# The preparation of a graph kernel in another order: histogram of 64 by 98 columns, projection spread over the statistics, scaling and turning between its last tiles

## The chip, the core and the metric

One core of a Trainium2 chip runs the kernel. It has a matrix engine (TensorE, PE in the profile), a vector engine (DVE), a scalar engine (ACT), GpSimd (POOL), an engine that only issues transfers (SP), and 16 DMA engines. Each engine works through its own list of instructions in order and waits on semaphores for the others. The metric is the time of one execution on the device in microseconds (us), lower is better; the figure of a kernel is the median of its timed runs.

## The reference

Two blocks of a graph network over 6250 nodes with 256 features and 100000 edges (sorted by their destination) are computed, each behind a layer norm and with a residual. The first has three hops of graph convolution, the second two layers of attention with four heads.

```python
h = jnp.maximum(_layernorm(x, axis=-1), 0.0)
x = x + _L0_gnn_ref(h, L0_gnn_W, L0_gnn_b, src, dst)
h = jnp.maximum(_layernorm(x, axis=-1), 0.0)
x = x + _L1_gnn_ref(h, edge_index, L1_gnn_W1, ..., L1_gnn_b2)

# _L0_gnn_ref
out_deg = jax.ops.segment_sum(ones, src, num_segments=N)
in_deg = jax.ops.segment_sum(ones, dst, num_segments=N)
out_norm = jnp.clip(out_deg, 1.0, None) ** (-0.5)
in_norm = jnp.clip(in_deg, 1.0, None) ** (-0.5)
h = x
for i in range(3):
    h = h * out_norm[:, None]
    h = jax.ops.segment_sum(h[src], dst, num_segments=N)
    h = h * in_norm[:, None]
    h = h @ W[i] + b[i]
    if i < 2:
        h = jax.nn.relu(h)
```

The change is confined to what comes before the first hop: the out-degree of every node (a histogram of 100000 numbers), the layer norm of x, and the product of its rows with the first weights, which the kernel takes ahead of the hop (sum and product may be exchanged).

## The kernel before

**Stages.** The nodes are 49 tiles of 128 rows (`NT`). The preparation fills the table `conv_tab[0]` in device memory with the scaled and projected rows. A hop then gathers, for each of 782 chunks of 128 edges, one row per edge from the table (POOL, L643) into a ring of 64 places; PE multiplies each with a one-hot matrix of destinations (L1015), and DVE adds the product to the sums of a tile in `acc` (L1303). Two more hops, two attention layers and the output follow. The change leaves them as they are.

**The histogram.** The source number of an edge is split into a low and a high part: `lo` = number mod 128, `hi` = number / 128. 800 columns of 125 edges are worked through in 40 halves of 20 columns (`HB`). For a half DVE makes the one-hot rows of both parts (L1171, two instructions, 128x20 and 49x20 elements of bf16), in one of two buffers. PE then runs 20 products of bf16 into the accumulator `psad` (L922): for column j the stationary operand is `oh_lo[:, b, :, j]`, 128 columns, and the moving one `oh_hi[:, b, :, j]`, 49 columns. The last index is the fastest one in memory and has 20 places, so both operands are read with a step of 20 elements, 40 bytes. DVE may fill a buffer again when PE has read it (semaphore `hist_done`), PE waits for `hist_onehots`. The result lies as 128 x 49, which is the layout of the tiles.

**Layer norm and projection.** x lies in `acc` (as `xa`). Per tile ACT takes mean and square sum (L706, L711), POOL subtracts the mean and clips at zero (L619, semaphore `x_ready`) and between its rows issues 14 gathers of index rows (L613). PE turns the tile by two transposes (`turn`, L936), ACT copies the turned tile from PSUM (L696), PE multiplies it with the weights (`multiply`, L944, two products in fp32 that the chip runs as four passes), and ACT copies the result back to `xa` (L719, semaphore `staged`). In ACT's own list the two copies of tile t stand right behind the statistics of tile t+3 and t+4, so statistics and projection go at one pace.

**The order of PE.** It is written out by hand. `HIST_LEAD` = 6: after every pair of halves (40 products) come two tiles, from the fourth pair on. 34 tiles are turned inside the histogram, 15 behind it.

**Behind the last tile.** DVE forms the out-norm and the factor `oscale` (L1219 to L1224, ACT takes the square root, L724), multiplies the projected rows by it in seven blocks (L1228, semaphore `ln_rows`), and SP stores each block when it is ready (L438). Then DVE prepares the chunk rows (L1233 to L1238), PE turns 14 blocks of them (L982, L988) and DVE copies each (L1241, L1244), packs tile numbers (L1250) and raises `steps_ready` (L1256). POOL's first gather waits for `steps_ready` and for all seven stores (`table_stored`). DVE waits for the stores too, clears `acc` in seven pieces (L1259) and starts the first hop.

Of the kernel before, what the change touches and what calls it, by code (L numbers as in the profile page):

```python
# [14 lines left out]
BF16 = mybir.dt.bfloat16  # L15
I32 = mybir.dt.int32
ALU = mybir.AluOpType
# [33 lines left out]
HIST_LEAD = 6  # L51
# [17 lines left out]
assert LP * LC == E and LC % (2 * HB) == 0 and NT % TB == 0 and S % 8 == 0 and U > LAG + 1 and S >= EC + NT - 1  # L69


def gnn(nc, x, src, dst, gw, gb, w1, as1, ad1, b1, w2, as2, ad2, b2, out):
    ctx = ExitStack()
    with ctx:
# [123 lines left out]
        o_lo, o_hi = 4 * LC, 4 * LC + HB * P  # L198
        oh_lo = ring[:, o_lo:o_hi].bitcast(BF16).rearrange("p (b n k) -> p b n k", b=2, k=HB)
        oh_hi = ring[:, o_hi:o_hi + HB * NT].bitcast(BF16).rearrange("p (b n k) -> p b n k", b=2, k=HB)  # L200
        o_c = o_hi + HB * NT
        iota_lo = ring[:, o_c:o_c + HB * P // 2].bitcast(BF16).rearrange("p (n k) -> p n k", k=HB)
        o_c += HB * P // 2
        iota_hi = ring[:, o_c:o_c + HB * NT // 2].bitcast(BF16).rearrange("p (n k) -> p n k", k=HB)
        o_c += HB * NT // 2
# [26 lines left out]
        o_c += 8 * SB + P + 2  # L232
        assert o_c <= RING * AW
# [157 lines left out]
        def _(sp):  # L391
# [44 lines left out]
            for q in range(NI):  # L436
                sp.wait_ge(ln_rows, TB * (q + 1))
# [133 lines left out]
        def _(pool):  # L571
            chain = [0]

            def link(ins):
# [9 lines left out]
            link(nc.gpsimd.iota(iota_lo, pattern=[[1, P], [0, HB]], base=0, channel_multiplier=0,  # L584
                                allow_small_or_imprecise_dtypes=True))
            nc.gpsimd.iota(iota_hi, pattern=[[1, NT], [0, HB]], base=0, channel_multiplier=0,
# [6 lines left out]
                                         base=0, pattern=[[-1, P]], channel_multiplier=1))  # L593
            link(nc.gpsimd.memset(ones[:, :], 1.0))
# [84 lines left out]
        def _(act):  # L679
# [18 lines left out]
            for s in range(NT + 4):  # L698
# [10 lines left out]
                if 0 <= t < NT:  # L709
# [3 lines left out]
                t = s - 3  # L713
                if 0 <= t < NT:
                    copy_rows_T(0, t)
                t = s - 4
                if 0 <= t < NT:
                    act.wait_ge(projected, t + 1)
                    nc.scalar.copy(xa[:, t, :], main[2 + t % 2][:, 0:C]).then_inc(staged, 1)  # L719
            chain[0] += NT  # L720
# [5 lines left out]
            root(norms[:, :], 1)  # L726
# [183 lines left out]
        def _(pe):  # L910
            pe.wait_ge(consts, 2)

            nc.tensor.matmul(psad[:, 0:NT], zero_b, zero_b[:, 0:NT], start=True, stop=False,
# [3 lines left out]
            def hist(first, end):  # L917
                for i in range(first, end):
# [39 lines left out]
            for i in range(NH):  # L958
# [6 lines left out]
                for t in (2 * i - HIST_LEAD, 2 * i + 1 - HIST_LEAD):  # L965
                    if t >= 0:
                        turn(0, t)
                    if t >= 1:
                        multiply(0, t - 1, wc, C)
# [772 lines left out]
```

## Time and profile before

| | us |
|---|---|
| median of 3 timed runs | 5737.9 (5733.7 to 5739.26) |
| the profiled execution | 5745.21 |
| its span in the profile | 5743.4 |
| PE busy | 3964.7 (69%) |
| POOL busy | 4134.0 (72%) |
| DVE busy | 3730.1 (65%) |
| ACT busy | 2157.1 (38%) |

The span reaches from the first to the last instruction of the profiled execution; 1.8 us of its time lie outside it. The profiled execution took 7.3 us more than the median. The preparation is the first 200 us, or 3.5% of the span. PE and PEld are two rows of one engine, products and loads of the stationary operand. The end of a matmul in the profile is modelled, its start is recorded, so the pace of PE is read from starts. PEclk is the granted clock of TensorE as a share of 2.4 GHz: 1.00 is 2.4 GHz, 0.50 is 1.2 GHz, and values between are a mix of the two in time.

### The profile page before, as it was taken

What the parts mean: (1) busy time and instruction counts of PE and PEld (TensorE: products, weight loads), DVE (VectorE), ACT (ScalarE), POOL (GpSimd) and SP (SyncE); (2) the same over time, 40 slices, a digit from 0 to 9 for tenths busy, and PEclk for the clock granted to TensorE, in tenths of its full rate; (3) what the DMA queues carried; (4) which work ended last, traced back from release to release, by engine and by line L of the source; (5) the groups of instructions that cost most, each with busy time, mean ns of one, the idle gap of its engine ahead of it and who ended that gap; (6) DMA issues with size and microseconds to landing.
All of it is one profiled execution on the core that took longest, in us unless ns stands there. A gap on an engine that the chain in (4) does not pass through costs nothing.

```text
span 5743.4 us, 108186 instructions
## 1 busy us (share of the span) xinstructions
PE 3964.7 (69%) x15160; PEld 2622.1 (46%) x15160; DVE 3730.1 (65%) x12287; ACT 2157.1 (38%) x7129; POOL 4134.0 (72%) x4290
## 2 busy tenths in 40 slices
PE   8566666676666667566666677777787677777772
PEld 8344444453344445343443454554554445444441
DVE  6556555555555554555555567777777677777777
ACT  3100000020000002000000088888888488888883
POOL 4577777777777777777777647777775577777775
PEclk8778777788777778777777788888888788898886
DMA  2443333333333333433333354444443344444444
GB/s 68 115 112 105 106 106 105 106 106 105 106 105 106 105 106 99 131 106 106 105 106 105 114 157 109 110 109 110 109 110 87 121 110 110 110 110 110 110 109 145
DMA packets 311837, 627.27 MB, mean 109 GB/s; under 512 B 87063, under 2 KB 182511, under 8 KB 311182
## 3 DMA queue, kind: packets, MB, share of 16 engines
q0 software_dynamic: 192928, 530.18, 33.4%
q1 hardware_dynamic: 111902, 88.77, 5.0%
q8 instruction: 222, 3.64, 0.3%
q14 instruction: 401, 3.28, 0.2%
q10 hardware_dynamic: 6384, 1.39, 0.2%
HBM read 573.49 MB, written 47.33 MB: 108 GB/s over the span
## 4 chain that ended last, share of the span: by engine, by line
PE 35%; DVE 19%; DMA 18%; issue 12%; POOL 11%; DVEq 3%; ACT 1%; POOLq 0%; SPq 0%; ACTq 0%
PE main L1015 20%; DMA ring<-conv_tab,csrc 14%; DVE acc L1303 8%; POOL ring L643 7%; PE main L1119 6%; PE main L944 4%; DMA ring<-attn_tab,sidx 4%; POOL ring L655 3%; DVEq L1303 2%; DVE ring L1631 2%; PE pso L1038 1%; PE psad L922 1%; POOL ring L675 1%; PE pso L936 1%; DVE ad L1525 1%
## 5 line engine op out<-in xcount | busy, mean ns | idle before, releaser
L643 POOL DMA_INDIRECT ring<-conv_tab,csrc x2346 | 2231.1, 951 | 729.8 <-issue 467.1
L1303 DVE TENSOR_TENSOR acc<-acc,main 128x264 f32 (+2 forms) x4160 | 1764.9, 424 | 1365.8 <-PE main L1015 963.6
L1015 PE MATMUL main<-ring,oh 128*128 x4992 | 1900.1, 538 | 1074.6 <-SPq L453 751.3
L655 POOL DMA_INDIRECT ring<-attn_tab,sidx x1664 | 1603.8, 964 | 624.2 <-issue 364.7
L1015 PEld LDWEIGHTS main<-ring,oh 128*128 128x128 f32 x4992 | 1226.8, 267 | 1744.6 <-issue 1539.2
L1119 PE MATMUL main<-ring,oh 128*128 128x264 f32 x3328 | 1211.7, 475 | 112.1 <-ACT ring L867 102.1
L867 ACT ACTIVATE ring<-ring 128x64 f32<-128x64 f32 x3328 | 918.9, 345 | 0.0
L1295 DVE TENSOR_SCALAR oh<-iota,dloc 128x128 f32<-128x128 f32 x2505 | 768.0, 307 | 169.7 <-issue 104.7
L1119 PEld LDWEIGHTS main<-ring,oh 128*128 128x128 f32 x3328 | 592.8, 220 | 262.3 <-DVE ring L1631 185.5
L845 ACT ACTIVATE oh<-iota,dloc 128x128 f32<-128x128 f32 x1752 | 558.0, 396 | 5.1 <-DMA attn_tab<-oh 5.1
L1631 DVE TENSOR_TENSOR ring<-ring 128x128 f32<-128x128 f32 x1670 | 467.8, 285 | 0.1
L797 ACT ACTIVATE nb<-acc,stat 128x256 f32<-128x256 f32 x49 | 24.5, 501 | 994.8 <-DVE stat L1403 994.8
L783 ACT ACTIVATE nb<-acc,inorm 128x256 f32<-128x256 f32 x49 | 24.3, 498 | 993.6 <-DVE acc L1303 993.3
L724 ACT ACTIVATE sdeg<-sdeg 128x49 f32<-128x49 f32 x1 | 0.2, 245 | 1016.3 <-DVE sdeg L1359 1016.3
L1038 PE MATMUL pso<-ident,oh 128*128 128x128 f32 x1744 | 334.5, 324 | 16.9 <-issue 7.9
L1055 PE MATMUL psad<-tvb,ohT_room 128*128 x1728 | 310.4, 189 | 46.8 <-ACT ohT_room L833 14.3
L833 ACT CAST ohT_room<-pso 128x512 bf16<-128x512 f32 x436 | 252.1, 578 | 169.7 <-PE pso L1038 168.9
L853 ACT ACTIVATE oh<-oh,ones 128x512 f32<-128x512 f32 x438 | 314.5, 718 | 0.7
L1055 PEld LDWEIGHTS psad<-tvb,ohT_room 128*128 128x128 bf16 x1728 | 184.1, 107 | 216.9 <-issue 145.7
L1038 PEld LDWEIGHTS pso<-ident,oh 128*128 128x128 f32 x1744 | 223.6, 164 | 46.0 <-issue 12.1
L675 POOL TENSOR_TENSOR ring<-ring,es 128x256 f32<-128x256 f32 x98 | 120.8, 1270 | 92.9 <-DMA ring<-attn_tab 92.9
L944 PE MATMUL main<-wc,aT 128*128 128x256 f32 x588 | 167.3, 412 | 0.7 <-DVE aT L1331 0.6
(210 smaller groups left out, 2815.6 us busy)
## 6 DMA issues: line engine op xcount, KB each, us to landing
ring<-conv_tab,csrc POOLq DMA_INDIRECT x2346, 2.8
ring<-attn_tab,sidx POOLq DMA_INDIRECT x1664
conv_tab<-oh SPq DMA_DIRECT2D x14, 896.0 KB, 4.0
ring<-attn_tab SPq DMA_DIRECT2D x14, 896.0 KB, 7.2
flag_room<-start_rows SPq DMA_DIRECT2D x424, 8.0 KB
flag_room<-end_rows SPq DMA_DIRECT2D x424, 8.0 KB
attn_tab<-ring SPq DMA_DIRECT2D x7, 910.0 KB, 4.4
attn_tab<-oh SPq DMA_DIRECT2D x7, 910.0 KB, 4.3
```

The costliest lines, as they stand in the source:

```text
L643: pool.indirect_dma_start(ring3[:, c % U, 0:C], None, conv_tab[k], bass.IndirectOffsetOnAxis(ap=csrc[:, c:c + 1], axis=0)).then_inc(gather ...
L655: pool.indirect_dma_start(ring3[:, j, 0:TW], None, attn_tab[l], bass.IndirectOffsetOnAxis(ap=sidx[:, i * GB * G + j:i * GB * G + j + 1], a ...
L845: sq = nc.scalar.activation(oh[:, (at + k) * P:(at + k + 1) * P], iota[:, :], ACT.Square, scale=-1.0, bias=dloc[:, col(k)])
L867: nc.scalar.activation(r, r, ACT.Copy, scale=ring3[:, b * G + k, C + h:C + h + 1]).then_inc(weighted_a, 1)
L944: mm = nc.tensor.matmul(main[t % 2 + (0 if m else 2)][:, 0:width], aT[:, (t % 2) * C + b * P:(t % 2) * C + (b + 1) * P], weights[:, b * wi ...
L1015: nc.tensor.matmul(main[s % 4][:, 0:width], oh[:, (s % OHR) * P:(s % OHR + 1) * P], ring[:, bass.ds(at, width)], start=True, stop=True).th ...
L1038: mm = nc.tensor.transpose(pso[q % 2][:, k * P:(k + 1) * P], oh[:, at * P:(at + 1) * P], ident[:, :])
L1055: mm = nc.tensor.matmul(psad[:, j * LW:(j + 1) * LW], ohT[:, ((q % 2) * 4 + k) * P:((q % 2) * 4 + k + 1) * P], tvb[:, bass.ds(t * LW, LW)] ...
L1119: nc.tensor.matmul(main[k % 4][:, 0:AW], oh[:, (b * G + k) * P:(b * G + k + 1) * P], ring3[:, b * G + k, :], start=True, stop=True).then_i ...
L1295: return nc.vector.tensor_scalar(oh[:, at * P:(at + 1) * P], iota[:, :], dloc[:, col], None, ALU.is_equal).then_inc(onehots, 1)
L1303: nc.vector.tensor_tensor(a, a, main[k][:, 0:width], ALU.add).then_inc(added, 1)
L1631: nc.vector.tensor_tensor(r, r, w.to_broadcast([P, DVEC // CH, CH]), ALU.mult).then_inc(weighted_v, 1)
```

## The change

The histogram is split 64 by 98: the low part has 64 values, the high part 98. The stationary operand has 64 columns and the moving one 98, still with a step of 40 bytes. The one-hot rows of a half have 162x20 elements where they had 177x20. The result lies as 64 x 98 and is brought to 128 x 49 by one copy and two small products with `ident` and `upper`.

The projection starts after the second half of the histogram, and runs one tile per three halves later. 19 tiles are turned inside the histogram, 30 behind it. ACT no longer ties one tile to one set of statistics: from tile 9 on it does four sets per tile. Its square root stands behind tile 21.

The rows of tiles 28 to 48 are scaled by ACT in the copy that it makes anyway; DVE scales the first 28 in four blocks, between its copies of turned chunk rows. PE turns the 14 blocks of chunk rows between its tiles 20 to 34. SP stores block q when its seven tiles are staged.

```diff
+LOW, HIGH = 64, 98
+T_EARLY = {1: 1, 2: 1, 3: 2, 4: 1, 5: 3}
+T_EVERY = 3
+T_ROOT = 21
+OWN = 4
-HIST_LEAD = 6
...
-                sp.wait_ge(ln_rows, TB * (q + 1))
+                if q < OWN:
+                    sp.wait_ge(ln_rows, q + 2)
+                else:
+                    sp.wait_ge(staged, TB * (q + 1))
...
+            def copy_projected(t):
+                act.wait_ge(projected, t + 1)
+                if t < OWN * TB:
                     nc.scalar.copy(xa[:, t, :], main[2 + t % 2][:, 0:C]).then_inc(staged, 1)
+                else:
+                    act.wait_ge(ln_rows, 1)
+                    nc.scalar.activation(xa[:, t, :], main[2 + t % 2][:, 0:C], ACT.Copy, scale=oscale[:, t:t + 1]
+                                         ).then_inc(staged, 1)
...
+                statistics(s)
+                if 3 <= s < 12 or (s >= 12 and s % 4 == 0):
+                    copy_rows_T(0, copied)
+                    if copied:
+                        copy_projected(copied - 1)
+                    copied += 1
...
+            def hist(i):
+                pe.wait_ge(hist_onehots, i + 1)
+                for j in range(HB):
+                    mm = nc.tensor.matmul(psad[0:LOW, 0:HIGH], oh_lo[:, i % 2, :, j], oh_hi[:, i % 2, :, j], start=False,
+                                          stop=False, skip_group_check=True)
+                mm.then_inc(hist_done, 1)
...
+            for i in range(2 * NH):
+                hist(i)
...
+                for _ in range(T_EARLY.get(i, int(i > 5 and i % T_EVERY == 2))):
+                    tile(t)
+                    t += 1
...
+            tile(t)
+            pe.wait_ge(hist_onehots, 2 * NH + 1)
+            nc.tensor.matmul(psb[:, 0:NT], ident[0:LOW, :], counts[:, 0:NT], start=True, stop=False)
+            nc.tensor.matmul(psb[:, 0:NT], upper, counts[:, NT:HIGH], start=False, stop=True).then_inc(hist_done, 1)
+            for n in range(NT - 1 - t):
+                tile(t + 1 + n)
+                if n < KB + SB:
+                    chunk_turn(n)
...
-            link(nc.vector.tensor_scalar(hi_i, lin, 7, None, ALU.arith_shift_right))
-            link(nc.vector.tensor_scalar(lo_i, lin, P - 1, None, ALU.bitwise_and))
+            link(nc.vector.tensor_scalar(hi_i, lin, 6, None, ALU.arith_shift_right))
+            link(nc.vector.tensor_scalar(lo_i, lin, LOW - 1, None, ALU.bitwise_and))
...
-                        for to, of, of_iota, n in ((oh_lo, lo_b, iota_lo, P), (oh_hi, hi_b, iota_hi, NT)):
+                        for to, of, of_iota, n in ((oh_lo, lo_b, iota_lo, LOW), (oh_hi, hi_b, iota_hi, HIGH)):
...
+            for b in range(1, KB):
                 dve.wait_ge(rowsT_done, b + 1)
                 nc.vector.tensor_copy(csrc[:, b * P:(b + 1) * P], main[b % 2][:, 0:P]).then_inc(rowsT_read, 1)
+                if b % 2 == 0:
+                    scale_rows(b // 2 - 1)
```

In the middle of the histogram PE's list before reads as follows. `psad` is the histogram, `pso` a turned tile, `main` a projected one, `ring` and `acc` hold one-hot rows and x; "x19" stands for 19 more of the same.

```order
L922 MATMUL psad<-ring 128x49 [waits hist_onehots]
L922 MATMUL psad<-ring 128x49 x19
L922 MATMUL psad<-ring 128x49 [waits hist_onehots]
L922 MATMUL psad<-ring 128x49 x19
L936 MATMUL pso<-ident,acc 128x128 [waits rows_T_copied,x_ready]
L936 MATMUL pso<-ident,acc 128x128
L944 MATMUL main<-wc,aT 128x256 [waits staged,rows_T_copied]
L944 MATMUL main<-wc,aT 128x256
```

At the same place the changed list has three halves, then one tile (its line numbers are those of the changed kernel).

```order
L951 MATMUL psad<-ring 64x98 [waits hist_onehots]
L951 MATMUL psad<-ring 64x98 x19
L951 MATMUL psad<-ring 64x98 [waits hist_onehots]
L951 MATMUL psad<-ring 64x98 x19
L951 MATMUL psad<-ring 64x98 [waits hist_onehots]
L951 MATMUL psad<-ring 64x98 x19
L965 MATMUL pso<-ident,acc 128x128 [waits rows_T_copied,x_ready]
L965 MATMUL pso<-ident,acc 128x128
L973 MATMUL main<-wc,aT 128x256 [waits staged,rows_T_copied]
L973 MATMUL main<-wc,aT 128x256
```

The number of products of the histogram is the same, their shape and what stands between them is not. Behind the histogram PE's list before ended with the last tile and then the chunk rows:

```order
L944 MATMUL main<-wc,aT 128x256 [waits staged,rows_T_copied]
L944 MATMUL main<-wc,aT 128x256
L982 MATMUL main<-ident,oh 128x128 [waits rowsf_ready,counts_read]
L982 MATMUL main<-ident,oh 128x128
L982 MATMUL main<-ident,oh 128x128 [waits rowsT_read] x5
L988 MATMUL main<-ident,oh 128x128 [waits rowsf_ready,rowsT_read]
```

Now each chunk row stands between two tiles (here the merge of the counts, tile 20, the first chunk block, tile 21, the second one):

```order
L1020 MATMUL psb<-ring,ident 128x49 [waits hist_onehots]
L1021 MATMUL psb<-ring 128x49
L965 MATMUL pso<-ident,acc 128x128 [waits rows_T_copied,x_ready]
L965 MATMUL pso<-ident,acc 128x128
L973 MATMUL main<-wc,aT 128x256 [waits staged,rows_T_copied]
L973 MATMUL main<-wc,aT 128x256
L1003 MATMUL main<-ident,oh 128x128 [waits rowsf_ready,counts_read]
L965 MATMUL pso<-ident,acc 128x128 [waits rows_T_copied,x_ready]
L965 MATMUL pso<-ident,acc 128x128
L973 MATMUL main<-wc,aT 128x256 [waits staged,rows_T_copied]
L973 MATMUL main<-wc,aT 128x256
L1003 MATMUL main<-ident,oh 128x128
```

The turning has moved from behind the last tile to places ahead of it. On DVE the list before had, behind the histogram, all seven scalings (`acc<-acc,oscale`) ahead of all chunk work:

```order
L1223 RECIPROCAL norms<-norms 128x98 [waits norm_sq]
L1224 TENSOR_TENSOR oscale<-norms 128x49 [waits dve_chain]
L1228 TENSOR_TENSOR acc<-acc,oscale 128x1792 [waits staged,dve_chain]
L1228 TENSOR_TENSOR acc<-acc,oscale 128x1792 [waits staged] x6
L1233 TENSOR_SCALAR oh<-csrc 128x896 [waits chunk_rows_in]
L1237 TENSOR_TENSOR oh<-oh 128x896 [waits dst_steps_in]
L1238 TENSOR_SCALAR oh<-oh 128x896 [waits dve_chain]
L1241 CAST csrc<-main 128x128 [waits rowsT_done] x7
L1244 COPY dloc<-main 128x128 [waits rowsT_done] x7
```

Now four scalings lie among the copies of the turned rows:

```order
L1280 CAST csrc<-main 128x128 [waits rowsT_done]
L1282 RECIPROCAL norms<-norms 128x98 [waits norm_sq]
L1283 TENSOR_TENSOR oscale<-norms 128x49 [waits dve_chain]
L1287 CAST csrc<-main 128x128 [waits rowsT_done,ln_rows]
L1287 CAST csrc<-main 128x128 [waits rowsT_done]
L1276 TENSOR_TENSOR acc<-acc,oscale 128x1792 [waits staged]
L1287 CAST csrc<-main 128x128 [waits rowsT_done] x2
L1276 TENSOR_TENSOR acc<-acc,oscale 128x1792 [waits staged]
L1287 CAST csrc<-main 128x128 [waits rowsT_done] x2
L1276 TENSOR_TENSOR acc<-acc,oscale 128x1792 [waits staged]
L1292 COPY dloc<-main 128x128 [waits rowsT_done] x7
L1276 TENSOR_TENSOR acc<-acc,oscale 128x1792 [waits staged]
```

Three of the seven scalings are gone from DVE.

## Rows read from the trace of the kernel before

**Rows 1.** Busy time by stretch: PE, PEld, DVE, ACT, POOL, PEclk, DMA share, GB/s.

```profile
32.50:148.50 116.00, 115.95 (x880) 106.41 (x881) 68.57 (x66) 50.61 (x196) 56.79 (x46) 0.80 0.04 9
148.50:171.20 22.70, 22.15 (x97) 13.98 (x95) 0.49 (x2) 21.04 (x86) 15.96 (x14) 1.00 0.00 1
```

**Rows 2.** Chain of waits, 165 to 190 us: start, us, what.

```profile
170.79 0.37 ACT acc L719
171.18 1.28 ACT L724
175.84 11.70 DVE acc L1228 x6
```

**Rows 3.** Timeline: first gather of the first hop.

```profile
199.72 1.03 POOL L643 DMA_INDIRECT ring<-conv_tab,csrc  x1 [0.78 <-POOL ring L660]
```

**Rows 4.** Groups, 220 to 1150 us: busy, mean ns, idle before.

```profile
L643 POOL DMA_INDIRECT ring<-conv_tab,csrc x740 | 704.9, 953 | 225.6 <-issue 145.7 <-PE main L1015 79.9
```

**Rows 5.** Timeline of PE around two pairs of halves: start, us.

```profile
32.51 4.04 PE L922 MATMUL psad<-ring 128*128 128x49 bf16 x40 [4.96 <-DVE ring L1171]
36.38 0.41 PE L936 MATMUL pso<-ident,acc 128*128 128x128 f32 x1
...
93.20 3.91 PE L922 MATMUL psad<-ring 128*128 128x49 bf16 x40
96.93 0.41 PE L936 MATMUL pso<-ident,acc 128*128 128x128 f32 x1
```

**Rows 6.** Busy time by stretch, inside these two pairs of halves.

```profile
32.50:36.40 3.90, 3.89 (x41) 3.78 (x42) 3.71 (x4) 0.00 (x0) 0.00 (x0) 0.50 0.06 2
93.20:96.60 3.40, 3.40 (x38) 3.40 (x37) 1.70 (x2) 1.82 (x8) 2.41 (x3) 1.00 0.00 0
```

**Rows 7.** Groups by form, 0 to 215 us.

```profile
L922 PE MATMUL psad<-ring 128*128 128x49 bf16 x800 | 78.7, 274 | 8.1 <-DVE ring L1171 8.0
L922 PEld LDWEIGHTS psad<-ring 128*128 128x128 bf16 x800 | 76.6, 147 | 11.3 <-DVE ring L1171 6.0 <-DMA wc<-in_L_gnn_W_dram 2.8 <-issue 0.9
L1171 DVE TENSOR_TENSOR ring<-ring 128x2560 bf16<-128x2560 bf16 x40 | 61.5, 1537 | 39.8 <-PE psad L922 39.7
L1171 DVE TENSOR_TENSOR ring<-ring 128x980 bf16<-128x980 bf16 x40 | 26.4, 660 | 0.0
L970 PE MATMUL psad<-ring 128*128 128x49 bf16 x1 | 0.2, 187 | 0.0
L970 PEld LDWEIGHTS psad<-ring 128*128 128x128 bf16 x1 | 0.1, 98 | 0.0
```

**Rows 8.** Groups by form on PEld, whole span: 64 stationary columns.

```profile
L1076 PEld LDWEIGHTS psb<-ones,do 1*64 1x64 f32 x212 | 22.2, 145 | 0.0
```

**Rows 9.** Chain of waits, 90 to 98 us: one tile on PE at either clock.

```profile
91.19 0.22 PE pso L936 x2
91.42 0.86 PE main L944 x4
...
97.11 0.45 PE pso L936 x2
97.56 1.71 PE main L944 x4
```

**Rows 10.** Timeline, 10 to 30 us: where the histogram begins.

```profile
10.72 4.05 DVE L1171 TENSOR_TENSOR ring<-ring 128x2560 bf16<-128x2560 bf16 x4
...
12.94 3.96 PE L922 MATMUL psad<-ring 128*128 128x49 bf16 x40 [2.74 <-DVE ring L1171]
...
21.24 1.45 PE L962 MATMUL main<-ring,ones 128*128 128x343 f32 x2
...
23.63 3.92 PE L922 MATMUL psad<-ring 128*128 128x49 bf16 x40
```

**Rows 11.** Transfers of the table: issue to landing.

```profile
DMA to landing us min/median/max: 4.4/6.5/9.3
```

More of the change, by code:

```diff
@@ L593, in _ @@
                                          base=0, pattern=[[-1, P]], channel_multiplier=1))
+            link(nc.gpsimd.memset(upper, 0.0))
+            link(nc.gpsimd.affine_select(out=upper, in_=upper, compare_op=ALU.not_equal, fill=1.0,
+                                         base=LOW, pattern=[[-1, P]], channel_multiplier=1))
             link(nc.gpsimd.memset(ones[:, :], 1.0))
@@ L696, in copy_rows_T, with statistics @@
                 nc.scalar.copy(aT[:, (t % 2) * C:(t % 2 + 1) * C], pso[t % 2][:, 0:C]).then_inc(rows_T_copied, 1)
-            for s in range(NT + 4):
+            def statistics(s):
                 t = s
@@ L724, in root @@
                 nc.scalar.activation(dst_, dst_, ACT.Sqrt).then_inc(norm_sq, 1)
-            root(norms[:, :], 1)
+            for t in range(copied, NT):
+                copy_rows_T(0, t)
+                copy_projected(t - 1)
+                if t == T_ROOT:
+                    root(norms[:, :], 1)
+            copy_projected(NT - 1)
             act.wait_ge(keys_ready, 1)
@@ L911, in _ @@
             pe.wait_ge(consts, 2)
[L913 removed]
+            nc.tensor.matmul(psad[0:LOW, 0:HIGH], zero_b[:, 0:LOW], zero_b[:, 0:HIGH], start=True, stop=False,
                              skip_group_check=True).then_inc(products_done, CR)
@@ L957, in _, with tile, chunk_turn @@
             pe.wait_ge(wc_in, 16)
-            for i in range(NH):
-                hist(i, i + 1)
-                if i == 1:
+            def tile(t):
+                turn(0, t)
+                if t:
+                    multiply(0, t - 1, wc, C)
+            def chunk_turn(n):
+                if n == 0:
+                    pe.wait_ge(counts_read, 1)
+                    pe.wait_ge(rowsf_ready, 1)
+                if n == KB:
+                    pe.wait_ge(rowsf_ready, 2)
+                if n >= 2:
+                    pe.wait_ge(rowsT_read, n - 1)
+                rows = b3(crowf)[:, n, :] if n < KB else b3(dl)[:, n - KB, :]
+                nc.tensor.transpose(main[n % 2][:, 0:P], rows, ident[:, :]).then_inc(rowsT_done, 1)
+            t = 0
+            for i in range(2 * NH):
+                hist(i)
+                if i == 3:
                     pe.wait_ge(chunks_ready, 1)
```

98 lines of the change are left out of this document (38 added, 60 removed).

## The prediction, written before the changed kernel was run

> **What bounds the kernel now.** I read the views in this order: busy shares by stretch, the chain of waits, the timeline of PE, the groups by form, and last the durations of single operations that the change moves.
>
> The busy shares come first because the change touches 200 us of 5743, and the reader must know which engine that part waits for. Between 32.5 and 148.5 us PE is busy for 115.95 of 116.00 us, DVE for 68.57, ACT for 50.61 and POOL for 56.79 [rows 1]. PE alone sets the pace of the histogram, and DVE stood 39.7 us in all before its one-hot instructions, waiting for PE to free a buffer [rows 7]. From 148.5 to 171.2 us the last 15 tiles run; PE is busy for 22.15 of 22.70 us and ACT for 21.04 [rows 1], so here statistics and copies on ACT run level with PE.
>
> The chain of waits shows what follows: ACT's copy of the last tile at 170.79, its square root with a table load of 1.28 us at 171.18, then DVE's scalings, 11.70 us for six of seven, from 175.84 on [rows 2]. Chunk rows are prepared, turned and packed behind them, and POOL's first gather starts at 199.72 [rows 3], 28.9 us after ACT has begun the last copy. In the first hop POOL is the bound: 740 gathers of 953 ns are 704.9 of 930 us, another 145.7 is time to issue them, and only 79.9 us is waiting for PE [rows 4]. So the end of the kernel moves by as much as the first gather, and the whole question is when that gather can start.
>
> **The price of a product of the histogram.** Everything hangs on this number, since there are 800 products before and after. 40 products starting at 93.20 are followed by the next instruction at 96.93: 3.73 us, 93 ns each. 40 starting at 32.51 are followed at 36.38: 3.87 us, 97 ns each [rows 5]. The granted clock was 1.00 in the first case and 0.50 in the second [rows 6]. An array that takes in a column per cycle would have doubled its time; this pace doesn't know the clock. Also 49 columns in 93 ns are 1.9 ns each, while the product of the tiles, read contiguously, follows the clock: 0.86 us at the one, 1.71 at the other for the same four instructions [rows 9]. The single product L970, with the same shape but contiguous operands, took 187 ns against a mean of 274 in the histogram, and its weight load 98 against 147 [rows 7]. What differs is the step of 40 bytes: reading an operand is the limit, not computing.
>
> A rule of the Trainium skill bears on it: "SBUF — State Buffer", section "Door 1: The DMA port swizzle", in its box on cachelines, says memory is read in lines of 16 bytes and a stride that enters a new line at every element pays at every element. Both operands do that here; the trace agrees as far as it goes, with its 93 ns at either clock.
>
> There are two operands, and only one can be the slower. Weights are loaded beside the product before. If the moving operand is the limit, 98 columns cost 98 x 1.9 = 186 ns a product. If the weights are, 64 columns instead of 128 make it cheaper or leave it. The durations speak for the moving one: strided, the product grows by 87 ns over L970, the load by 49 [rows 7], and the load has room beside a product of 274. The nearest row of 64 stationary columns is L1076, 145 ns a load in fp32 [rows 8], below 186. I take 186 ns. The ends are 93 (a price for each pair) and 194 (twice the 97).
>
> The Trainium skill, "TensorE: Matmul & The Clock Gate", section "Weight-path perf modes — Fast Weight Load (FWL) and DoubleRow", adds that the fast load wants 128 weights and a type other than fp32, which 64 columns give up. By its section on LDWEIGHTS the load would be an estimated 53 ns at 1.2 GHz without the stride, still under the moving stream; the sum stays as it is.
>
> **The change part by part.**
>
> *Histogram.* A half costs 20 x 186 = 3.73 us instead of 1.87, 40 halves 149.2 us instead of 74.6.
>
> *DVE.* Its half has 162x20 elements per partition for 177x20. From 1537 and 660 ns for 2560 and 980 elements [rows 7], 0.555 ns an element, it falls from 2.02 (two halves in 4.05, [rows 10]) to 1.87 us, which a half of PE of 3.73 us covers. If PE's half stays at 1.87, the cover is gone and both run level.
>
> *Start.* PE's first product stays at 12.94 [rows 10], and so do the products that count the edges, from 21.24 to 23.63, 2.4 us [rows 10]. The waits for DVE in the first halves (8.0 us in all, [rows 7]) vanish, because the histogram is slower.
>
> *Tiles inside.* 18 whole tiles and the first turn of the next. A tile is 1.08 us at 2.4 GHz (0.22 + 0.86) and 2.16 us at 1.2 GHz (0.45 + 1.71) [rows 9]. Before, 34 tiles took what 116 us leave after 680 products (63.5) and 4.96 us of waiting [rows 5]: 1.40 us each. The granted clock fell after stretches with histogram alone (the tiles at 97.11 are at 1.2 GHz, those at 91.19, with tiles right before, not). Now 11.2 us of histogram lie between single tiles, so I expect more of them at the low clock: 1.77, the middle. 18 x 1.77 + 0.4 = 32.3 us. ACT and POOL were busy for about half of these 116 us [rows 1] and do the same work in a longer stretch.
>
> *End of the histogram.* 12.9 + 149.2 + 2.4 + 32.3 = 196.8 us. Before it was 148.5.
>
> *Behind it.* Tile 19 and the merge: 2.1 + 0.5. The merge is what DVE's copy and two products of 49 columns cost; no row shows them, bounds are 0.2 (one contiguous product, L970) and 1 us, and part lies under tile 19. 29 tiles at 1.08, since ACT has no statistics left: 31.3. 14 turns of chunk rows, between 0.11 and 0.22 us each by the turn of a tile at either clock [rows 9]: 0.15, 2.1. The last product's end to its copy 0.9. Stalls: the square root with its 1.28 us stands between ACT's copies [rows 2], DVE's scalings of 1.95 us (11.70 / 6) between the copies of chunk turns; two PSUM buffers cover part; 2 us, bounds 0 and 5. Sum 38.9, so PE ends at 235.7.
>
> *To the gather.* ACT copy 0.4 (0.37 in [rows 2]), the last store from issue to landing 4.4 us (the least of seven, since nothing runs beside it, [rows 11]; the median 6.5 would be 2 more), POOL's start 0.4: 240.9 us. The square root, 14 us of scaling, the chunk rows and the packing, which filled the 28.9 us after the last tile, are done ahead of it or beside it. The chunk rows are turned by tile 34, so their packing ends before the last store. DVE's clearing of `acc` still waits for the stores, as before.
>
> *Sum.* First gather 240.9 against 199.7: +41.2 us. On the profiled execution 5745.2 + 41.2 = 5786.4. That execution is 7.3 us above the median of the runs shown, so on the median 5737.9 + 41.2 = 5779.1. Split: +74.6 for the products, -26.3 for 15 tiles fewer inside the histogram and its waits for DVE, +16.6 for the tiles behind it (38.9 for 22.3), -23.7 for the tail (5.2 for 28.9). The reordering saves, the split costs more. The two are even where a product costs 186 - 41.2/0.8 = 134 ns.
>
> **The rivals.**
>
> *B, the price is per product.* 93 ns stays whatever the columns: histogram 74.6, 18 tiles at 1.40 and 0.4, end at 12.9 + 74.6 + 2.4 + 25.6 = 115.5, and 44.1 us as above to the gather: 159.6, that is -40.1, 5697.8 on the median. This ends on the other side. For it speaks that the pace was the same at two clocks and that 128 stationary columns halved to 64 could pay for the doubled moving side. Against it, the L970 row: its 49 columns without a step are faster, so columns count. It decides if the price stays under 134 ns.
>
> *C, a pair has a part of both.* Weights and moving operand share the reading, or the limit is the load of 64 columns: about 130 ns a product. 800 x 56 ns less: -45, 5734. For it: 145 ns of L1076 [rows 8] lies near, and a load of 147 ns on average isn't far from hidden. Against: the load starts with the product before it and needs less than that.
>
> *D, PE is no longer the bound.* If half the stationary columns relieve it, DVE is left: 10.7 [rows 10] + 40 x 1.87 + 10 for its other work (what the 137.8 us from there to 148.5 leave after 87.9 of one-hot rows and 39.8 of waiting, [rows 7]) = 95.5 us, gather at 139.6, -60, 5678. The back-to-back rule of the Trainium skill, "TensorE: Matmul & The Clock Gate", would allow PE a product in an estimated 43 ns at 98 columns; the pace of 93 with 49 speaks against it.
>
> **How the numbers follow.** Forecast A 0.76, B 0.12, C 0.08, D 0.04. A's own range: with 175 ns a product (a fixed part of 12) -9, tiles at 1.40 -7, tiles at 2.16 and 3 us more of stalls +10, 194 ns a product +6; not all at once, so 5764 to 5792. The range for all goes down to C, 5732, and up to 5794; B, D and a tail above are left out, 0.2. A measurement of this kernel tells about 0.2% from no change, so "same" is 5726.4 to 5749.4: half of C and a little of A, 0.05. Faster: B, D and the rest of C, 0.19. Slower 0.76.
>
> **What would show it.** In the profile after: 20 products of the histogram take 3.7 us (B: 1.9, C: 2.6). DVE's one-hot instructions wait for PE some 1.8 us a half, 70 us in all. The histogram ends near 197, tiles inside it run partly at 1.2 GHz, those behind it at 1.1 us apiece. The first gather is near 241 and no scaling or turning stands behind the last tile. Everything from there on is as before, shifted. I am wrong if a histogram product is below 134 ns, or if the chain of waits shows ACT or DVE between the tiles behind the histogram for more than 5 us.

## The result and the profile after

The changed kernel takes 5781.78 us in the median of four runs (5776.1 to 5782.94), the kernel before 5737.73 (5733.7 to 5739.26, with one run more than in the table of before): a ratio of 1.0076, 95% interval 1.006 to 1.0092. It is 44.05 us slower; 5779.1 was forecast. The profiled execution took 5781.07 us, with a span of 5779.3.

Busy time by stretch of the changed kernel, columns as in [rows 1]. The stretches are the start, the rest of the histogram, and the tiles behind it:

```profile
12.90:32.50 19.60, 19.60 (x92) 16.94 (x93) 10.58 (x12) 5.20 (x22) 7.30 (x5) 1.00 0.90 295
32.50:200.10 167.60, 167.60 (x826) 151.56 (x824) 71.65 (x88) 51.13 (x208) 77.71 (x58) 0.56 0.03 6
200.10:240.50 40.40, 39.54 (x203) 32.75 (x202) 17.15 (x32) 23.35 (x63) 0.52 (x1) 0.92 0.41 137
```

PE is busy without a gap from 12.9 to 200.1 us. The granted clock of 0.56 in the long stretch, against 0.80 in [rows 1], says that nearly all of it ran at 1.2 GHz. The groups by form, 0 to 260 us, answer to [rows 7]:

```profile
L951 PE MATMUL psad<-ring 128*64 128x98 bf16 x800 | 146.1, 358 | 1.8 <-DVE ring L1211 1.8
L951 PEld LDWEIGHTS psad<-ring 128*64 128x64 bf16 x800 | 140.5, 195 | 11.2 <-DVE ring L1211 7.8 <-DMA wc<-in_L_gnn_W_dram 1.8 <-issue 1.6
L1211 DVE TENSOR_TENSOR ring<-ring 128x1960 bf16<-128x1960 bf16 x40 | 47.1, 1177 | 0.0
L1211 DVE TENSOR_TENSOR ring<-ring 128x1280 bf16<-128x1280 bf16 x40 | 33.8, 846 | 96.0 <-PE psad L951 96.0
```

The products' waits for DVE went from 8.0 to 1.8 us, and DVE's wait for PE from 39.7 to 96.0. The timeline of PE shows a period of the histogram, three halves and a tile:

```profile
183.12 10.90 PE L951 MATMUL psad<-ring 128*64 128x98 bf16 x60
193.95 0.69 PE L965 MATMUL pso<-ident,acc 128*128 128x128 f32 x2
194.43 1.92 PE L973 MATMUL main<-wc,aT 128*128 128x256 f32 x4
196.28 3.79 PE L951 MATMUL psad<-ring 128*64 128x98 bf16 x20
199.89 0.26 PE L1016 MATMUL psad<-ring 128*64 128x98 bf16 x1
```

Sixty products take 193.95 - 183.12 = 10.83 us, 180.5 ns each; they took 93 before. The tile takes 196.28 - 193.95 = 2.33 us. From the seventh half on the histogram repeats this period.

The tail, from the chain of waits (start, us, what), answers to [rows 2]:

```profile
206.46 1.16 PE main L973 x4
207.62 0.02 issue
207.65 0.03 ACT acc L732
207.67 0.36 issue
208.04 0.82 ACT L750
208.86 0.47 issue
209.33 0.28 ACT norms L750
209.62 0.27 ACT aT L709
...
238.70 1.75 PE main L973 x8
240.45 0.03 issue
240.48 0.48 ACT acc L735
240.96 0.02 issue
240.98 4.41 DMA conv_tab<-acc
```

The square root with its table load costs PE one gap of 0.8 us and is then out of the way. After the last tile there is one copy, the last store of 4.41 us, and the first gather, which the timeline puts at 246.11 us ([rows 3] had 199.72):

```profile
246.11 1.03 POOL L656 DMA_INDIRECT ring<-conv_tab,csrc  x1 [17.48 <-DMA conv_tab<-acc]
```

So 46.4 us are lost ahead of the first gather, and the medians differ by 44.05. The two profiled executions differ by less, 35.9 us. The first store of the attention table stands at 3307.81 us before and at 3344.14 after, that is 36.3 later:

```profile
3307.81 0.37 SPq L448 DMA_DIRECT2D attn_tab<-ring  x1
```

```profile
3344.14 0.37 SPq L458 DMA_DIRECT2D attn_tab<-ring  x1
```

The 10 us between lie in the hops, which the change doesn't touch. The profiled execution of before was 7.3 us above its median, and most of the 10 us is that: from the first gather to the end of the span it took 5543.7 us, the changed kernel 5533.2, and the profiled executions of e1_reorder_alone, e2_split_alone and e4_tiles_behind below 5533.2, 5532.0 and 5536.4.

### The profile page after: what moved, and what is told of

Read it like the earlier page. It is cut to its first block, busy times and chain, and to the rows that moved or that the text cites. A ratio compares the mean times of both kernels' runs of the same rounds, so it can differ in the third digit from the quotient of the medians.

```text
span 5779.3 us, 108210 instructions
## 1 busy us (share of the span) xinstructions
PE 4058.9 (70%) x15164; PEld 2703.7 (47%) x15164; DVE 3719.5 (64%) x12285; ACT 2159.7 (37%) x7129; POOL 4129.0 (71%) x4292
## 4 chain that ended last, share of the span: by engine, by line
PE 35%; DVE 18%; DMA 18%; issue 13%; POOL 11%; DVEq 4%; ACT 1%; POOLq 0%; SPq 0%; ACTq 0%
PE main L1055 20%; DMA ring<-conv_tab,csrc 15%; DVE acc L1353 8%; POOL ring L656 7%; PE main L1159 5%; PE main L973 4%; POOL ring L668 3%; DMA ring<-attn_tab,sidx 3%; PE psad L951 3%; DVEq L1353 3%; DVE ring L1681 2%; PE pso L1078 1%; POOL ring L688 1%; PE pso L965 1%; DVE ad L1575 1%
## 5 line engine op out<-in xcount | busy, mean ns | idle before, releaser
L1159 PE MATMUL main<-ring,oh 128*128 128x264 f32 x3328 | 1233.3, 482 | 111.9 <-ACT ring L898 99.4
L1078 PEld LDWEIGHTS pso<-ident,oh 128*128 128x128 f32 x1744 | 225.5, 166 | 48.2 <-issue 15.2
```

What stands on the lines that cost most here:

```text
L1078: mm = nc.tensor.transpose(pso[q % 2][:, k * P:(k + 1) * P], oh[:, at * P:(at + 1) * P], ident[:, :])
L1159: nc.tensor.matmul(main[k % 4][:, 0:AW], oh[:, (b * G + k) * P:(b * G + k + 1) * P], ring3[:, b * G + k, :], start=True, stop=True).then_i ...
```

## The experiments

The runs stand in three groups, e1 to e4, e5 to e8 and e9 to e11, each on one chip with the kernel before beside it. On the second and the third chip the whole kernel took about 7.3 ms, before and changed alike: the trace of e5 moved 85 GB/s where 109 were moved on the first chip, and the time was lost in the hops. In the preparation a product took 93 ns and a tile 1.09 us there, as on the first chip. So for these runs the first gather, from the trace, is the sharper measure, and the differences in time have some 15 us of scatter. The kernel before has no trace on these two chips; its 199.7 us are those of [rows 3].

| | time, us | before, same chip | difference | ratio, 95% interval | first gather, us |
|---|---|---|---|---|---|
| before | | | | | 199.7 |
| changed | 5781.8 | 5737.7 | +44.1 | 1.006 to 1.0092 | 246.1 |
| e1_reorder_alone | 5708.1 | 5734.1 | -26.0 | 0.9938 to 0.9971 | 171.6 |
| e2_split_alone | 5817.3 | 5734.1 | +83.2 | 1.0127 to 1.0161 | 282.9 |
| e4_tiles_behind | 5760.6 | 5734.1 | +26.5 | 1.0026 to 1.0059 | 223.8 |
| e5_128x49_tiles_behind | 7351.8 | 7359.2 | -7.4 | 0.9972 to 0.9996 | 178.0 |
| e6_128x49_8_inside | 7331.2 | 7359.2 | -28.0 | 0.9945 to 0.9974 | 170.8 |
| e7_8byte_step_128x49 | 7316.6 | 7359.2 | -42.7 | 0.9921 to 0.9954 | 147.8 |
| e8_8byte_step_64x98 | 7322.1 | 7359.2 | -37.1 | 0.9928 to 0.9962 | 159.3 |
| e9_8byte_30_inside | 7243.6 | 7299.9 | -56.3 | 0.9905 to 0.995 | 147.2 |
| e10_8byte_128x49_again | 7251.7 | 7299.9 | -48.2 | 0.9909 to 0.9949 | 149.7 |
| e11_8byte_64x98_again | 7257.0 | 7299.9 | -42.9 | 0.9924 to 0.9964 | 160.1 |

**e1_reorder_alone.** The changed kernel with one part undone.

```diff
-LOW, HIGH = 64, 98
+LOW, HIGH = 128, 49
```

> The changed order of the preparation, with the histogram split 128 by 49 again. If a product costs what it cost before (93 ns) and tiles between histogram halves stay at 1.2 GHz (2.33 us each, as in the changed kernel), the histogram ends 800 x 87 ns = 70 us earlier, near 130 us, and the first gather is near 176 us: 5781.8 - 70 = 5712 us, range 5703 to 5724. If the order alone were worth nothing (the tiles at the low clock eat what the tail gives back), 5738 us.

It took 5708.13 us, 26.0 below the kernel before. The order alone is a gain; the split turned it into a loss. The difference to the changed kernel is 70.1 us in the time and 74.5 at the first gather. Counted on PE from each start to the next, the products with their waits for DVE make 63.8 of the 74.5 (144.8 us against 81.0), the tiles inside 6.7 (39.7 against 33.0) and what stands behind the histogram 3.7. The 800 products at 87 ns each would be 70; 4.0 us of what is missing are waits for DVE, which come back with the cheaper product.

**e2_split_alone.** The kernel before with the other part.

```diff
+LOW, HIGH = 64, 98
-mm = nc.tensor.matmul(psad[:, 0:NT], oh_lo[:, b, :, j], oh_hi[:, b, :, j], start=False,
+mm = nc.tensor.matmul(psad[0:LOW, 0:HIGH], oh_lo[:, b, :, j], oh_hi[:, b, :, j], start=False,
...
+                if t == 2 * NH - HIST_LEAD:
+                    pe.wait_ge(hist_onehots, 2 * NH + 1)
+                    nc.tensor.matmul(psb[:, 0:NT], ident[0:LOW, :], counts[:, 0:NT], start=True, stop=False)
+                    nc.tensor.matmul(psb[:, 0:NT], upper, counts[:, NT:HIGH], start=False, stop=True
+                                     ).then_inc(hist_done, 1)
```

> The order before, with the histogram split 64 by 98 and its result brought to 128 by 49 by one copy and two small products. The 800 products cost 87 ns more each (+70 us), the 5 us of waits for DVE go, the merge costs 1 to 2: 5804 us if the 34 tiles inside stay at 1.40 us each; if the longer histogram between them keeps them at 1.2 GHz (2.16 to 2.33 us) up to 32 us more, 5836. I expect 5815. If the price of the split came from the new order and not from the shape of the product, 5740.

It took 5817.32 us, and its first gather stands at 282.93 us, 83.2 later; the time is 83.2 us longer. The two parts alone add up to +57.2 and together give +44.05; at the first gather it is +55.1 and +46.4. The split costs more where more tiles stand inside the histogram: counted in the same way, it made the 34 tiles of the old order dearer by 16.5 us (52.6 to 69.1) and the 19 of the new one by 6.7. Busy time of this run, histogram and the tiles behind it, in the columns of [rows 1]:

```profile
32.50:215.00 182.50, 181.69 (x842) 160.92 (x841) 66.79 (x80) 46.74 (x179) 47.69 (x43) 0.67 0.03 5
```

The 34 tiles inside ran at 1.2 GHz far more often than before: the clock of the stretch is 0.67 against 0.80 in [rows 1].

**e3_prices.** Batches of 40 products at the head of TensorE's list, twice over. The added function, with m and n the stationary and moving columns, ms and ns the steps in elements:

```diff
+            def price(m, ms, n, ns):
+                w = flat[:, 0:m * ms].rearrange("p (n k) -> p n k", k=ms)
+                x = flat[:, 0:n * ns].rearrange("p (n k) -> p n k", k=ns)
+                for j in range(40):
+                    nc.tensor.matmul(psb[0:m, 0:n], w[:, :, j % ms], x[:, :, j % ns], start=True, stop=True)
+                nc.tensor.matmul(psb[:, 0:2], ident[:, :], ident[:, 0:2], start=True, stop=True)
```

> The changed kernel with 16 batches of 40 bf16 products added at the head of TensorE's list, twice over, on tables of numbers, each batch with its own number of stationary and moving columns and step in memory; their results go nowhere. Only the pace of the batches is read. Theory 1, the moving operand read with a step of 40 bytes sets the price (1.85 ns a column): 64 by 98 costs 180 ns whether the weights have a step or not, and under 60 once the moving operand is contiguous; 64 by 49 costs 93 as 128 by 49 does; 128 by 98 costs 180; 64 by 128, 236; 98 by 64, 120. Theory 2, the load of 64 strided weights sets it (they lose the fast load): 64 by 98 stays near 180 with a contiguous moving operand and falls under 95 with contiguous weights; 64 by 49 costs 180; 128 by 98 stays near 93. Theory 3, both add up: taking the step from either saves about half.

Four batches of the second pass from the timeline of PE, each followed by the small fp32 product that ends it:

```profile
102.50 7.35 PE L957 MATMUL psb<-ring 128*64 128x98 bf16 x40
109.78 0.59 PE L958 MATMUL psb<-ident 128*128 128x2 f32 x2
110.30 7.21 PE L957 MATMUL psb<-ring 128*64 128x98 bf16 x40
117.44 0.59 PE L958 MATMUL psb<-ident 128*128 128x2 f32 x2
117.96 4.86 PE L957 MATMUL psb<-ring 128*64 128x98 bf16 x40
122.74 0.59 PE L958 MATMUL psb<-ident 128*128 128x2 f32 x2
123.26 3.47 PE L957 MATMUL psb<-ring 128*64 128x98 bf16 x40
126.67 0.59 PE L958 MATMUL psb<-ident 128*128 128x2 f32 x2
```

They have the same shape, 64 by 98, and all four ran at 1.2 GHz. In the first both operands have the step of 40 bytes, in the second only the moving one, in the third only the stationary one, in the fourth neither. From the start of a batch to the product behind it: 7.28, 7.14, 4.78 and 3.41 us. All batches, as the mean distance between the starts of two products in the second pass (the first pass agrees within 1 ns but for one batch), both operands with a step of 40 bytes where nothing else is said:

| stationary x moving | ns a product |
|---|---|
| 64 x 98 | 179 |
| 64 contiguous x 98 | 176 |
| 64 x 98 contiguous | 117 |
| 64 x 98, both contiguous | 82 |
| 128 x 49 | 93 |
| 128 contiguous x 49 | 89 |
| 128 x 49 contiguous | 60 |
| 128 x 49, both contiguous | 41 |
| 64 x 49 | 119 |
| 128 x 98 | 180 |
| 64 x 128 | 232 |
| 98 x 64 | 176 |
| 64 contiguous x 98 with a step of 4, 8, 16, 32 bytes | 78, 89, 175, 179 |

The second pass ran at a granted clock of 0.50, but for the steps of 4 bytes (0.53), 8 bytes (1.00) and 16 bytes (0.66). The two batches with everything contiguous go at the pace of that clock: 98 / 1.2 = 82 ns, 49 / 1.2 = 41 ns. So does the step of 4 bytes, which took 82 ns at 0.50 in the first pass. These three are bounds set by the clock, not by reading; what they would cost at 2.4 GHz no batch shows.

Theory 1 holds for the changed shape: take the step from the weights and nothing changes, take it from the moving operand and the price falls by a third. The moving operand costs 89 / 49 = 176 / 98 = 232 / 128 = 1.81 ns a column. Theory 1 had put it under 60 ns with a contiguous moving operand; it is 117, and 82 even with both contiguous, at 1.2 GHz. Theory 2 is right in one thing that theory 1 missed. The load of 64 strided weights costs 117 ns, and that of 128 only 60. It lies hidden under 180 here, but it is what 64 by 49 pays (119, not the 93 I expected) and 98 by 64 (176, not 120). Theory 3 is out.

The price of the loads bears on a rule that the prediction weighed: by the Trainium skill, "TensorE: Matmul & The Clock Gate", section "Weight-path perf modes — Fast Weight Load (FWL) and DoubleRow", only 128 weights get the fast load. The trace agrees: 64 and 98 strided weights cost the same 1.81 ns a column as the moving operand (117 and 176 ns), 128 cost 0.47.

**e4_tiles_behind.** The changed kernel, all tiles behind the histogram.

```diff
-                for _ in range(T_EARLY.get(i, int(i > 5 and i % T_EVERY == 2))):
-                    tile(t)
-                    t += 1
...
-            tile(t)
+            for t in range(TURNED + 1):
+                tile(t)
```

> The changed kernel with all 49 tiles turned and projected behind the histogram, none inside; ACT takes all statistics first. If the 18 tiles inside cost 2.33 us because TensorE's clock is at 1.2 GHz after 11 us of histogram, and cost 1.09 us in a row behind it, this gives 18 x 1.24 = 22 us, less some 4 us until the clock rises and something for the queue of ACT: 5763 us, range 5756 to 5772. If tiles cost the same wherever they stand, 5782.

It took 5760.56 us, 26.5 above the kernel before where the changed kernel was 44.05 above; the first gather came 22.3 us earlier than in the changed kernel, of which 17.6 are seen in the times. Busy time in the histogram and in the tiles, columns as in [rows 1]:

```profile
45.00:159.00 114.00, 114.00 (x645) 113.87 (x644) 59.36 (x62) 11.03 (x50) 62.50 (x49) 0.50 0.05 8
165.00:215.00 50.00, 49.20 (x278) 41.81 (x277) 16.13 (x29) 31.21 (x88) 0.52 (x1) 1.00 0.34 111
```

The histogram runs wholly at 1.2 GHz, and the tiles at 2.4 GHz; a tile inside costs 2.33 us, one in the row behind 1.09.

**e5_128x49_tiles_behind and e6_128x49_8_inside.** Both have 128 by 49. The first has no tile inside the histogram, the second only the eight early ones. The line shown is that of the second; the first leaves the whole loop out.

```diff
-                for _ in range(T_EARLY.get(i, int(i > 5 and i % T_EVERY == 2))):
+                for _ in range(T_EARLY.get(i, 0)):
```

> The reordered kernel with 128 by 49 (run e1_reorder_alone) and all 49 tiles behind the histogram. The histogram alone is then bound by DVE: 10.7 + 40 x 2.04 + about 10 for its other work = 102 us, 49 tiles of 1.09 and 14 chunk turns of 0.11 make 55, merge, end and store 8: first gather near 165 against 171.6 in e1_reorder_alone, so some 6 us below its time. If the low clock inside the histogram cost nothing, because TensorE waited for DVE anyway, it would be slower by the 49 - 30 = 19 tiles less the 27 us that the histogram gets shorter, that is about the same time.

> As e5_128x49_tiles_behind, but 8 tiles stand early inside the histogram, where DVE is busy with the index work and TensorE would wait. They should be free: histogram end 102 to 107 us, 41 tiles behind it, first gather near 160: 5 to 10 us below e5_128x49_tiles_behind. If the early tiles push the histogram back by their own 2.2 us each (8 x 2.2 = 17), it is 8 us above it.

Both missed their numbers, by 13 and 11 us of first gather. The difference between them, 7.2 us, is in the range that was expected, but the eight early tiles were not free: the histogram ended at 115.5 us with them and at 113.1 without, and 2.4 us more lie in a longer wait of the first (below), so they cost 2.4 to 4.8 us inside and saved about 9 behind. The miss of both is in DVE. The timeline of PE in the first:

```profile
102.75 4.06 PE L946 MATMUL psad<-ring 128*128 128x49 bf16 x40 [0.21 <-DVE ring L1202]
106.98 2.06 PE L946 MATMUL psad<-ring 128*128 128x49 bf16 x20 [0.17 <-DVE ring L1202]
109.26 4.04 PE L946 MATMUL psad<-ring 128*128 128x49 bf16 x40 [0.21 <-DVE ring L1202]
113.12 0.22 PE L1007 MATMUL psad<-ring 128*128 128x49 bf16 x1
```

Three halves take 109.26 - 102.75 = 6.51 us, 2.17 each, where I had reckoned with the 2.04 of the first halves; over 40 halves that is 5 us. Another 5.8 us is a single wait, ahead of the half at 46.33 us, that the profile puts down to no engine of this core. The traces of e6_128x49_8_inside and e1_reorder_alone have one too, of 3.41 us at 46.12 and 1.69 at 44.54; what it was stays open.

```profile
46.33 6.32 DVE L1202 TENSOR_TENSOR ring<-ring 128x2560 bf16<-128x2560 bf16 x6 [5.80 <-remote]
```

Moving the tiles out gives nothing with 128 by 49: 178.0 against 171.6 us with 19 inside (e1_reorder_alone). With no tile inside PE waits 15.7 us for DVE within the histogram, with 19 inside 4.0, so the tiles lie partly in that wait.

**e7_8byte_step_128x49, e8_8byte_step_64x98, and again e10 and e11.** The one-hot rows in groups of four edges, so that the step is 8 bytes; the work of DVE and PE is otherwise the same.

```diff
+KI = 4
-        oh_lo = ring[:, o_lo:o_hi].bitcast(BF16).rearrange("p (b n k) -> p b n k", b=2, k=HB)
+        oh_lo = ring[:, o_lo:o_hi].bitcast(BF16).rearrange("p (b g n k) -> p b g n k", b=2, g=HB // KI, k=KI)
...
-                    mm = nc.tensor.matmul(psad[0:LOW, 0:HIGH], oh_lo[:, i % 2, :, j], oh_hi[:, i % 2, :, j], start=False,
+                    mm = nc.tensor.matmul(psad[0:LOW, 0:HIGH], oh_lo[:, i % 2, j // KI, :, j % KI],
+                                          oh_hi[:, i % 2, j // KI, :, j % KI], start=False,
```

> The reordered kernel with 128 by 49 and another layout of the one-hot rows: groups of four edges, so that TensorE reads both operands with a step of 8 bytes instead of 40. By the batches (89 ns for 64 by 98 at 8 bytes, 41 for 128 by 49 with no step) a product falls from 93 to 45 to 60 ns, TensorE gets room for the tiles inside and DVE becomes the bound, if its instructions keep their 2.04 us a half in the new layout: histogram end 102 to 105 instead of 129, first gather near 146, about 26 us below e1_reorder_alone. If DVE loses its fast pace in runs of four elements (some 3.6 us a half), the histogram ends near 165 and the kernel is 36 us above e1_reorder_alone.

> The changed kernel as it is, 64 by 98, with the same layout in groups of four edges and nothing else changed. If the step of 40 bytes is what makes the products dear, they fall from 180 to 89 ns, the histogram ends near 129 instead of 200 us, and the time falls by 71 us against the changed kernel, to some 26 below the kernel before. If the price belonged to the shape 64 by 98, nothing would move.

> The kernel of e7_8byte_step_128x49 again, on another chip if it comes to that, for a tighter ratio: first gather at 147.8 us against 199.7 before, 52 us, so 0.991 where the kernel before takes 5734 us, 5682 us.

> The kernel of e8_8byte_step_64x98 again: first gather at 159.3 us, 40 us before that of the kernel before and 87 before that of the changed kernel: 5694 us where the kernel before takes 5734.

e8 is the changed kernel but for this layout, and its timeline of PE answers to the period shown above:

```profile
107.23 3.80 PE L952 MATMUL psad<-ring 128*64 128x98 bf16 x40
111.40 1.99 PE L952 MATMUL psad<-ring 128*64 128x98 bf16 x20 [0.37 <-DVE ring L1213]
113.33 0.44 PE L967 MATMUL pso<-ident,acc 128*128 128x128 f32 x2
113.60 1.03 PE L975 MATMUL main<-wc,aT 128*128 128x256 f32 x4
114.56 1.99 PE L952 MATMUL psad<-ring 128*64 128x98 bf16 x20
```

Forty products and the wait for DVE behind them take 4.17 us where forty took 7.22; a product alone takes 91 ns. The tile takes 1.23 us instead of 2.33. The first gather is at 159.3 us (e11: 160.1), 87 us before that of the changed kernel; I had forecast 71. The products with their waits gave 65 (144.8 to 79.4), and the tiles inside 17 (39.7 to 22.7), because they ran at 2.4 GHz. Busy time of e8 inside the histogram, columns as in [rows 1]:

```profile
45.00:119.00 74.00, 71.47 (x670) 63.37 (x668) 59.33 (x63) 41.02 (x169) 69.62 (x42) 1.00 0.05 13
```

With 128 by 49 (e7) a product falls to 49 ns and DVE becomes the bound, busy for 58.87 of 60.00 us:

```profile
45.00:105.00 60.00, 50.37 (x619) 42.49 (x618) 58.87 (x56) 40.08 (x166) 55.78 (x28) 0.68 0.04 10
```

DVE takes 2.15 us a half, as in e5 (2.17). The runs of four elements did it no harm: 1551 ns for 2560 elements where it was 1537 [rows 7]. The first gather is at 147.8 us (e10: 149.7) where 146 was forecast.

**e9_8byte_30_inside.** The kernel of e7 with eleven more tiles inside, and what follows from that: ACT copies four tiles per seven sets of statistics, its square root stands behind tile 32, and DVE scales five blocks.

```diff
-T_ROOT = 21
-OWN = 4
+T_ROOT = 32
+OWN = 5
...
-                if 3 <= s < 12 or (s >= 12 and s % 4 == 0):
+                if 3 <= s < 12 or (s >= 12 and 4 * s % 7 < 4):
...
-                for _ in range(T_EARLY.get(i, int(i > 5 and i % T_EVERY == 2))):
+                for _ in range(T_EARLY.get(i, int(i > 5 and i % T_EVERY > 0))):
...
+                    scale_rows(4)
```

> Run e7_8byte_step_128x49 (128 by 49, step of 8 bytes) with two tiles per three halves instead of one, 30 inside the histogram and 19 behind it. There DVE set the pace (busy for 58.9 of 60 us) and TensorE was busy for 50.4, so part of the eleven further tiles, 1.1 to 2.2 us each, has to be paid: histogram end 105 to 115 us instead of 105, 12 us fewer behind it. First gather 138 to 148 against 147.8: 0 to 10 us below e10_8byte_128x49_again. If ACT, whose statistics and copies fill two thirds of that stretch, or GpSimd (55.8 of 60 us) becomes the bound, no gain.

The first gather came at 147.18 us, 2.5 before e10's and 0.6 before e7's, near the small end of the gain that was expected. The eleven tiles cost nothing inside: the histogram ended at 105.6 us, as in e7 (105.1). But behind it PE waits for POOL, 8.8 us in all:

```profile
108.11 0.44 PE L967 MATMUL pso<-ident,acc 128*128 128x128 f32 x2 [1.00 <-POOL acc L633]
...
112.18 0.44 PE L967 MATMUL pso<-ident,acc 128*128 128x128 f32 x2 [0.97 <-POOL acc L633]
...
120.41 0.44 PE L967 MATMUL pso<-ident,acc 128*128 128x128 f32 x2 [1.10 <-POOL acc L633]
```

The subtraction of the mean on POOL (21.00 of 21.00 us busy from 115 on) is now the bound; its last one ends at 136.5 us, and only then can PE turn the last tile. e9 and e10 are the fastest versions: 0.9927 and 0.9929 of the kernel before, each with an interval of about 0.002. They are not told apart.

## Why the prediction was right

**The price of a product** was forecast at 186 ns and measured at 180.5, for the reason given: the moving operand is read with a step of 40 bytes at 1.81 ns a column. e3_prices shows it for the product alone, and e8_8byte_step_64x98 in the kernel. The term was 149.2 us and is 144.4. The argument from [rows 5 and 6], a pace that does not know the clock, was sound: in the changed kernel sixty products took 10.83 us at a granted 0.73 (from 51.71 us) and 10.83 at 0.50 (from 78.00). The 4.8 us too many come from charging all of the 93 ns to the columns; 89 belong to them.

**The two parts.** "The reordering saves, the split costs more" is shown by e1_reorder_alone (-26.0) and e2_split_alone (+83.2). The forecast implied -33.4 for the order, 41.2 less 74.6; at the first gather it is -28.1. The forecast let all waits for DVE vanish, which holds with the dear product alone; with 128 by 49 PE waits 4.0 us for DVE inside the histogram.

**The tiles inside** are the term that was mis-sized. I took 1.77 us, midway between the prices at the two clocks; it was 2.3 in 13 of the 18. Two steps failed here. The first is the clock: I had read that tiles keep the high level when other tiles stand right before them, from those at 91.19 us. But the chain of waits has histogram products right before them:

```profile
89.98 1.21 PE psad L922 x13
```

Forty products stood before both these tiles and those at 97.11, and the one pair ran at 2.4 GHz, the other at 1.2. So the rows gave no rule to place the tiles between the two levels, and the middle was a guess. With sixty products of 180 ns between single tiles, all eleven of the period ran at 1.2 GHz. The second is the 0.17 us by which they exceed the 2.16 of [rows 9]. With 128 by 49 a tile between histogram products took 2.13 at the same clock (e1_reorder_alone), so the excess comes with the split. Most of it lies behind the tile: the load of 64 weights for the next product of the histogram starts 0.56 us after the tile's last product has begun (104.29 against 103.73 us), while e1_reorder_alone loads its 128 weights beside that product and goes on after 0.43. Why 64 columns are not loaded beside it stays open.

All 18 and the first turn took what 200.1 - 12.9 us leave after 144.4 of products and 2.4 of counting, 40.4 us against 32.3. With the 4.8 too many above, the histogram ended at 200.1 where 196.8 was forecast. The 1.40 us that I had read for a tile of the kernel before are wrong as well: I took off the 4.96 us of waiting, which lie ahead of 32.51 us and so outside the 116 us. The tiles cost 52.5 / 34 = 1.54. This changes the price of rival B by some 3 us and not the forecast.

**Behind the histogram** 38.9 us were forecast and 40.4 measured: the clock stayed low until 207 us (tiles of 2.32, 2.19 and 1.62 us, of which the sum had only the first at the low clock), the merge took 1.0 us for 0.5, and of the 2 us set aside for stalls the square root took one gap of 0.8. The scalings of DVE cost nothing. The tail came to 5.7 us against 5.2, with the last store at 4.41.

**The sum** was +41.2 at the first gather; it is +46.4: the tiles inside took 8.1 us more than forecast, the products 4.8 less, what stands behind 1.9 more. The time moved by 44.05, within the range. That it landed 2.7 us from the forecast owes something to luck: the products put too dear made good 4.8 of the 8.1 us by which the tiles were put too cheap, and +46.4 at the gather appeared as +44.05 in the medians.

**The rivals.** B, one price whatever the columns, is refuted by 180.5 ns. C named the load of 64 weights at about 130 ns, and it does cost 117: the forecast was right that it lies hidden, not that it is harmless. D, DVE as the bound, didn't come; DVE waited 96.0 us for PE, more than the 70 I named.

## What to carry to other kernels

Where a matmul's pace doesn't change with the clock, suspect the reading of an operand, and count the columns of each operand with their own price: here 1.81 ns for each moving column at a step of 16 bytes or more, and as much for each stationary one with 64 or 98 of them at 40 bytes. Try the step before the shape; here groups of four elements left the writer's speed alone and halved the product. A reordering and a resizing in one change should be timed apart, since here one gained 26 us and the other lost 70.

## What the runs showed of the hardware

The step has an edge between 8 and 16 bytes: for 98 moving bf16 columns 8 bytes cost 89 ns, at a granted 1.00 as at 0.81 in the first pass, 16 bytes 175 and 32 bytes 179. That fits the rule on lines of 16 bytes named in the prediction (the Trainium skill, "SBUF — State Buffer", section "Door 1: The DMA port swizzle"): at 8 bytes every second element enters a new line, at 16 each one does. The same box has two reads of a line suffice for the full rate, and that is not so here: at 8 bytes a column took 0.91 ns at 2.4 GHz, where one a clock would be 0.42.

Fewer stationary columns can be dearer: with a step of 40 bytes and 49 moving columns, 64 of them cost 119 ns and 128 cost 93.

A busy PE in the profile is not one that keeps its clock. In the histogram of e4_tiles_behind PE was busy for 114.00 of 114.00 us at a granted clock of 0.50, in that of e8_8byte_step_64x98 for 71.47 of 74.00 at 1.00. The products have the same shape in both; they follow each other in 180 ns in the first and in 91 in the second, and tiles stand among them in the second alone. The tiles are not what keeps the clock up: the changed kernel has them at the same places as e8_8byte_step_64x98, differs from it in the step alone, and was granted 0.56 in its long stretch. Nor does the step of 8 bytes suffice: e7_8byte_step_128x49, with products of 49 ns and 1.0 us of waiting in each period of 6.5, was granted 0.68, and most of its tiles took the 2.17 us of the low clock. What the clock goes by stays open.

The durations of the tiles bear the rows out: the first four products with the projection weights behind the histogram of e4_tiles_behind took 1.86 us, those inside e8_8byte_step_64x98 0.96. They are the surer reading: for 12.90 to 32.50 us of the changed kernel the row says 1.00, while the same products at 24.95 us took 1.84 us, the time of the low clock.
